# Windowed attention on quarter tiles: row-quarter scores, channel-major attended values, weights normalised before the transpose

## The chip, the core and the metric

One core of a Trainium2 chip runs the whole program. The time is device microseconds from start to end, the median of several executions. A profile is one further execution, taken by the hardware profiler. TensorE (PE) multiplies from SBUF into PSUM banks; VectorE (DVE), ScalarE (ACT) and GpSimd (POOL) do the elementwise work; SyncE (SP) issues the transfers. Each engine works through its own instructions in order and waits on semaphores for the others. TensorE's clock has two levels, 2.4 and 1.2 GHz, which the profile shows as a granted clock of 1.00 or 0.50.

## The reference

A network of five parts on 64 x 8192 inputs; after the first, each adds its result to h (64 sequences of 128 positions with 64 channels, float32). The change concerns the second part, windowed attention with eight heads of eight channels. A window is one sequence of 128 positions:

```python
qkv = xw @ qkv_weight.T + qkv_bias
q, k, v = (qkv[0], qkv[1], qkv[2])
attn = jnp.einsum('whqd,whkd->whqk', q * scale, k)
attn = attn + jnp.transpose(rpb, (2, 0, 1))[None]
attn = jax.nn.softmax(attn, axis=-1)
out = jnp.einsum('whqk,whkd->wqhd', attn, v).reshape(Bb * nW, WINDOW, C)
out = out @ proj_weight.T + proj_bias
```

The other parts are a convolutional tokenizer with its own attention, a slice attention, a bidirectional GRU with gates, and eight experts of which two are used.

## The kernel before

The stages run one after the other: 1a and 1b (convolutions and channel attention), 2 (this attention), 3 (slice attention), 4 and 5 (norm and GRU), 6 (gates), 7 (experts). Two sequences lie side by side in one 128-partition tile, a lane `l`; 32 such pairs make the stage. `stage2_pe`, `stage2_dve`, `stage2_act` and `stage2_pool` are the four engines' programs. Each has a function `slot(i, t)` that is run for t = 0 to 7 in 17 rounds i by `pipelined` (GpSimd has a loop of its own). A slot is a unit: a quarter of the 2 x 8 heads of a pair, so four heads and their 128 x 512 scores; four slots are one pair, and a round two. The order within a slot is fixed by hand, and each engine handles in one slot units of different age: `back(i, t, d)` names the unit d slots ago.

For a pair, GpSimd scales the centred rows of h (`rows`, L504), TensorE transposes them (L552), ScalarE copies them (L622), and TensorE makes queries, keys and values (L558 to L560). GpSimd spreads the keys: for each unit it multiplies them with a mask so that each head's rows stand alone in a 128 x 512 tile (`spread`, L512). For a unit, TensorE multiplies queries and spread keys (L571), VectorE adds the position bias and finds the smallest value, the scores being negated (L679), ScalarE takes the exponential in place (L646), TensorE transposes the four 128 x 128 weights into one of banks 4 to 7 (L583), VectorE copies them out (L688), and TensorE multiplies them with the values (L608). The values carry a column of ones per head, so that product also gives the softmax sum; VectorE takes its reciprocal (L697) and scales the heads' results (L700). Once a pair TensorE transposes those (L592), ScalarE copies (L656), TensorE projects and adds the bias (L598, L599), and VectorE adds to h (L692). `centre`, `square`, `variance` and `rsqrt` prepare the next stage's norm once a round.

Of the kernel before, what the change touches and what calls it, by code (L numbers as in the profile page):

```python
# [59 lines left out]
def build(nc, xp, consts, out):  # L60
# [109 lines left out]
    def stage1a_dve(v):  # L170
# [9 lines left out]
        def turn(i, g):  # L180
            if g == 0:
                max1(i, 1)
                if isinstance(i, int) and i == JA // 2 - 1:

                    v.wait_ge(loaded, 16)
                    setup3_rows_dve(v)

                    nc.vector.tensor_scalar(a_bqs[:, :], c("a_bq"), -HD ** -0.5, None, ALU.mult).then_inc(a_setup, 1)
                    nc.vector.tensor_scalar(c("a_bias"), c("a_bias"), -1.0, None, ALU.mult).then_inc(a_setup, 1)
            elif not isinstance(i, int) or i < JA // 2 - 1:  # L190
                max1(i + 1, 0)
            else:
                setup3_middle_dve(v)
# [262 lines left out]
    a_v = lane(512, 2 * 168)  # L456
    a_kz = lane(1024, 2048)
    a_o, a_oT = lane(5136, 128), lane(5264, 128)
# [27 lines left out]
    def pipelined(engine, slot):  # L486

        for t in range(8):
            slot(0, t)
        with engine.Fori(1, N2 - 1) as i:  # L490
# [6 lines left out]

    def stage2_pool(pool):
        def rows(i, l, first=False):
            n = i * 2 + (l + 1)  # L500
            if not first:
# [5 lines left out]
        def spread(i, l):  # L507


            for u in range(4):  # L510
                pool.wait_ge(a_k_r, i * 2 + (l + 1))
                nc.gpsimd.tensor_tensor(a_kz[l][:, 512 * u:512 * (u + 1)].rearrange("p (h k) -> p h k", h=4),  # L512
                                        a_k[l].unsqueeze(1).to_broadcast([128, 4, 128]),
                                        c("a_mask", 4 * u, 4 * u + 4).unsqueeze(2).to_broadcast([128, 4, 128]), ALU.mult).then_inc(a_kz_r, 1)
# [4 lines left out]

        rows(0, 0, True)  # L520
        rows(0, 1, True)
        spread(0, 0)
        for i in (1, 2):
            rows(i, 0)
            spread(i - 1, 1)
            rows(i, 1)
            spread(i, 0)
        with pool.Fori(3, N2) as i:
            finish(i - 3)
            rows(i, 0)  # L530
            spread(i - 1, 1)
            rows(i, 1)
            spread(i, 0)
        spread(N2 - 1, 1)

        pool.wait_ge(ln_rstd, LN[1] + 1)
        pool.wait_ge(a_t_r, NP)
        pool.wait_ge(f_still, 4)
        stage3_pool(pool, start=0)
        finish(N2 - 3)  # L540
        finish(N2 - 2)
        stage3_pool(pool, start=1)
        finish(N2 - 1)

    def stage2_pe(pe):
        def rows(i, l):
# [4 lines left out]
            pe.wait_ge(a_oT_r, i * 2 + (l + 1))  # L551
# [9 lines left out]

        def slot(i, t):
            l, u = t // 4, t % 4
            if exists(i, 0):
                if u == 0:
                    pe.wait_ge(a_q_r, i * 2 + (l + 1))
                pe.wait_ge(a_kz_r, i * 8 + (t + 1))
                if t >= 2 or exists(i, -1):

                    pe.wait_ge(a_mx_r, i * 8 + (t - 1))  # L570
# [1526 lines left out]
```

## Time and profile before

| | |
|---|---|
| median of 3 executions | 1465.39 us (1465.26 to 1466.63) |
| the profiled execution | 1466.03 us, span 1464.2 us |
| busy share of the span | PE 92%, DVE 66%, ACT 54%, POOL 39% |
| stage 2 | first row transposes at 231.6 us, last projection at 580.3 us |
| mean granted clock | 0.949 |

TensorE records every float32 product as two matmuls and a float32 transpose as one. A record's duration includes its way through the array; the next starts before it ends, so the pace is read from start to start. The same holds, to a smaller degree, for ScalarE and VectorE. A number behind x counts records.

### The profile page before, as it was taken

To read this page: it belongs to the slowest core of one execution; us is meant where nothing else is said; L and a number is where in the kernel's file an instruction comes from. 1 tells how busy PE (TensorE), PEld (TensorE's weight loads), DVE (VectorE), ACT (ScalarE), POOL (GpSimd) and SP (SyncE) were. 2 spreads that over 40 slices of the span, in tenths; PEclk is the share of its full clock that TensorE was granted. 3 is DMA by queue.
4 is the path that set the end of the run, shared out by engine and by line. 5 is a ranking of instruction groups with operands and counts; after the bars stand their busy time and mean duration, and the time that the engine had idled before them with its cause. 6 is when DMAs were issued, how large, how long until landed. Compare 5 with 4: busy or idle time off the path is not lost.

```text
span 1464.2 us, 42346 instructions
## 1 busy us (share of the span) xinstructions
PE 1352.3 (92%) x15300; PEld 969.4 (66%) x15300; DVE 969.7 (66%) x3518; ACT 788.6 (54%) x2105; POOL 569.1 (39%) x902
## 2 busy tenths in 40 slices
PE   6998998999999997999999998899999999969997
PEld 2446876777777776777777776456666665446665
DVE  3775776888888887687887785235555555646664
ACT  3974664556555554445545544235555555634553
POOL 5000114454445453355565554213333333225554
PEclk9988998999999998999999999569999999969999
DMA  8300000000000000000000000000000000000001
GB/s 223 74 1 0 1 1 1 1 0 0 0 0 0 0 0 1 2 2 0 0 0 0 0 0 2 0 1 1 0 0 0 0 0 1 1 1 10 15 14 23
DMA packets 9965, 13.76 MB, mean 9 GB/s; under 512 B 9008, under 2 KB 9008, under 8 KB 9392
## 3 DMA queue, kind: packets, MB, share of 16 engines
q1 hardware_dynamic: 9904, 12.93, 3.6%
q8 instruction: 40, 0.66, 0.2%
q14 instruction: 21, 0.17, 0.0%
HBM read 10.83 MB, written 2.10 MB: 9 GB/s over the span
## 4 chain that ended last, share of the span: by engine, by line
PE 75%; DVE 11%; issue 6%; ACT 6%; POOL 1%; DMA 1%; DVEq 0%; ACTq 0%; POOLq 0%; SPq 0%
PE bank L608 7%; PE bank L1267 6%; PE bank L571 6%; PE bank L1604 4%; PE bank L1622 4%; PE bank L145 4%; PE bank L1261 4%; PE bank L583 3%; PE bank L956 3%; PE bank L1226 3%; PE bank L1291 2%; PE bank L983 2%; PE bank L323 2%; PE bank L164 2%; PE bank L1369 2%
## 5 line engine op out<-in xcount | busy, mean ns | idle before, releaser
L512 POOL TENSOR_TENSOR big<-big,cst 128x512 f32<-128x512 f32 x128 | 131.9, 1062 | 131.7 <-DVE big L669 131.7
L646 ACT ACTIVATE big<-big 128x128 f32<-128x128 f32 x512 | 160.3, 391 | 33.6 <-DVE big L679 33.6
L679 DVE CUSTOM_DVE_ANT_0 big<-bank,cst 128x128 f32<-128x128 f32 x512 | 117.7, 285 | 43.3 <-issue 43.3
L571 PE MATMUL bank<-big 128*128 128x512 f32 x256 | 135.9, 613 | 1.7 <-POOL big L512 1.7
L608 PE MATMUL bank<-big 128*128 128x96 f32 x1024 | 132.2, 272 | 0.0
L608 PEld LDWEIGHTS bank<-big 128*128 128x128 f32 x1024 | 124.3, 192 | 0.9 <-issue 0.8
L1339 POOL TENSOR_TENSOR big<-g_a,g_b 64x64 f32 x128 | 40.1, 313 | 189.9 <-DVE g_a L1329 189.9
L878 POOL TENSOR_TENSOR big<-big 128x512 f32<-128x512 f32 x64 | 65.6, 1045 | 117.4 <-DVE big L1132 117.4
L1658 ACT ACTIVATE big<-bank 128x512 f32<-128x512 f32 x128 | 66.2, 603 | 51.9 <-PE bank L1604 51.9
L1320 DVE SCALAR_TENSOR_TENSOR g_t<-bank,cst,g_r 128x64 f32<-128x64 f32 x128 | 36.3, 283 | 85.6 <-ACT g_r L1306 85.6
L583 PEld LDWEIGHTS bank<-cst,big 128*128 128x128 f32 x512 | 62.5, 141 | 43.4 <-issue 37.6
L1525 POOL TENSOR_TENSOR big<-big 128x512 f32<-128x512 f32 x48 | 61.0, 1270 | 76.2 <-DVE big L1728 73.5
L266 POOL TENSOR_TENSOR eps_var<-rowsq,eps 128x4 f32 (+3 forms) x48 | 9.6, 200 | 207.6 <-DVE rowsq L262 207.6
L1291 PE MATMUL bank<-cst 128*128 128x256 f32 (+1 forms) x256 | 88.3, 426 | 0.0
L688 DVE COPY big<-bank 128x512 f32<-128x512 f32 x128 | 87.6, 684 | 0.1
L1306 ACT ACTIVATE g_r<-bank,g_bias 128x64 f32<-128x64 f32 x128 | 40.1, 313 | 87.5 <-PE bank L1267 87.5
L1267 PEld LDWEIGHTS bank<-g_b,cst 128*64 128x64 f32 x1024 | 40.3, 136 | 60.3 <-DVE g_b L1327 59.9
L1082 ACT COPY big<-bank 128x512 f32<-128x512 f32 x64 | 38.2, 597 | 73.6 <-PE bank L965 73.6
L583 PE MATMUL bank<-cst,big 128*128 128x128 f32 x512 | 77.3, 273 | 0.0
L1622 PEld LDWEIGHTS bank<-cst,big 128*64 128x64 f32 x2048 | 63.4, 140 | 19.3 <-issue 17.4
L145 PE MATMUL bank<-big,w1s 96*128 96x512 f32 x128 | 61.1, 634 | 13.8 <-DMA big<-x_dram 11.9
L1261 PE MATMUL bank<-big,cst 128*128 (+1 forms) x192 | 67.6, 440 | 1.4 <-ACT big L1235 1.4
(265 smaller groups left out, 3428.3 us busy)
## 6 DMA issues: line engine op xcount, KB each, us to landing
big<-x_dram SPq DMA_DIRECT2D x12, 512.0 KB, 8.2
cst<-consts_dram SPq DMA_DIRECT2D x1, 3364.5 KB, 22.8
out_dram<-h SPq DMA_DIRECT2D x8, 256.0 KB, 2.6
cst<-consts_dram SPq DMA_DIRECT2D x3, 256.0 KB
cst<-consts_dram SPq DMA_DIRECT2D x1, 279.5 KB, 3.9
cst<-consts_dram SPq DMA_DIRECT2D x8, 2.0 KB
cst<-consts_dram SPq DMA_DIRECT2D x2, 4.0 KB
```

The costliest lines, as they stand in the source:

```text
L145: m = nc.tensor.matmul(T(0, 2 * (q % 2) + b), w1s[0:96, 128 * g:128 * (g + 1)], xin[w][:, (2 * q + b) * 512:(2 * q + b + 1) * 512], start= ...
L512: nc.gpsimd.tensor_tensor(a_kz[l][:, 512 * u:512 * (u + 1)].rearrange("p (h k) -> p h k", h=4), a_k[l].unsqueeze(1).to_broadcast([128, 4, ...
L571: nc.tensor.matmul(bank(t % 2), a_q[l], a_kz[l][:, 512 * u:512 * (u + 1)], start=True, stop=True).then_inc(a_sc_r, 1)
L583: m = nc.tensor.transpose(bank(4 + tb % 4)[:, 128 * k:128 * (k + 1)], a_P[tb % 4][:, 128 * k:128 * (k + 1)], eye)
L608: m = nc.tensor.matmul(bank(4 + tb % 4)[:, 96 * k:96 * (k + 1)], a_PT[tb % 4][:, 128 * k:128 * (k + 1)], a_v[tb // 4][:, at + 9 * k:at + 9 ...
L646: m = nc.scalar.activation(P, P, ACT.Exp, bias=a_mx[tb % 4][:, k:k + 1], scale=-1.0)
L679: m = nc.vector.tensor_tensor_reduce(a_P[t % 4][:, 128 * k:128 * (k + 1)], bank(t % 2)[:, 128 * k:128 * (k + 1)], c("a_bias", 512 * (u % 2 ...
L688: nc.vector.tensor_copy(a_PT[tb % 4], bank(4 + tb % 4)).then_inc(a_ptc_r, 1)
L1261: nc.tensor.matmul(T(group, gate)[:, w * half:w * (half + 1)], c("g_ih", 128 * gate, 128 * gate + 128), big1[:, bass.ds(first * B + w * ha ...
L1267: m = nc.tensor.matmul(to[64 * d:64 * d + 64, :], c("g_hh", 128 * gate + 64 * d, 128 * gate + 64 * d + 64), state[:, :], start=start, stop ...
L1291: nc.tensor.matmul(T(1 - u, 3)[:, 128:384 if more else 512], c("g_hh", 0, 128), c("m_w1", 0, 256 if more else 384), start=True, stop=True, ...
L1622: m = nc.tensor.matmul(out_bank(e)[64 * half:64 * half + 64, 64 * (2 * p + s):64 * (2 * p + s) + 64], hidden(e, s)[:, 128 * p + 64 * half: ...
```

## The change

Everything is within stage 2 and its constants.

- **Scores.** GpSimd multiplies the keys with a mask of four columns (`a_mask4`) once a pair, and the result serves all four units. A unit's scores are one matmul of 32 rows, the quarter u of queries and keys. They go to banks 0, 1, 5, 7 in turn, and are issued two at a time in the odd slots, one and two slots ahead.
- **Softmax.** ScalarE's exponential also writes its sum. VectorE takes the reciprocal one slot after the scores' minimum, and GpSimd scales the weights in place (`normed`) before they are transposed.
- **Transposes.** All go to bank 4. VectorE copies the even units' out, ScalarE the odd ones'.
- **Attended values.** The values lie zero-padded in 32 columns a head. Four matmuls a unit write the four column quarters of bank 6, channel by position; the transpose of the heads is gone. ScalarE copies the 128 x 512 once a pair.
- **Projection.** It takes that layout with padded weights (`a_proj_padded`), in eight matmuls of 64 x 64; GpSimd has added the bias to h beforehand, ahead of its row scaling.
- **Setup.** Eight small transfers for the padded weights, one memset, one mask sum.

```diff
-    a_v = lane(512, 2 * 168)
-    a_kz = lane(1024, 2048)
...
+    a_v, a_kz = lane(512, 512), lane(1024, 512)
+    a_oT = lane(1536, 512)
     def four(at, cols):
         return [big[k // 2][:, at + cols * (k % 2):at + cols * (k % 2 + 1)] for k in range(4)]
-    a_P, a_PT, a_mx, a_rs = four(3072, 512), four(4096, 512), four(5120, 4), four(5128, 4)
-    a_bqs, a_pb = sb("a_bqs", [128, 1]), sb("a_pb", [128, 128])
...
+    a_P, a_PT, a_mx, a_rs, a_sm = four(3072, 512), four(4096, 512), four(5120, 4), four(5128, 4), four(5136, 4)
...
-    def pipelined(engine, slot):
-        for t in range(8):
...
+    def pipelined(engine, slot, ahead=1):
+        for i in range(ahead):
+            for t in range(8):
+                slot(i, t)
+        with engine.Fori(ahead, N2 - 1) as i:
...
+    SBANK = (0, 1, 5, 7)
+    def scores_bank(t):
+        return bank(SBANK[t % 4])
     def stage2_pool(pool):
         def rows(i, l, first=False):
             n = i * 2 + (l + 1)
+            hp = h[:, bass.ds(i * 4 + 2 * l, 2), :]
+            nc.gpsimd.tensor_tensor(hp, hp, a_pb[:, :].rearrange("p (b c) -> p b c", c=C), ALU.add)
...
-            for u in range(4):
-                pool.wait_ge(a_k_r, i * 2 + (l + 1))
...
+            pool.wait_ge(a_k_r, i * 2 + (l + 1))
+            if l or exists(i, -1):
+                pool.wait_ge(a_sc_r, i * 8 + 4 * l)
+            nc.gpsimd.tensor_tensor(a_kz[l].rearrange("p (h k) -> p h k", h=4), a_k[l].unsqueeze(1).to_broadcast([128, 4, 128]),
+                                    a_m4[:, :].unsqueeze(2).to_broadcast([128, 4, 128]), ALU.mult).then_inc(a_kz_r, 1)
+        def normed(i, t):
+            pool.wait_ge(a_rs_r, i * 8 + (t + 1))
+            P = a_P[t % 4].rearrange("p (j k) -> p j k", j=4)
+            nc.gpsimd.tensor_tensor(P, P, a_rs[t % 4].unsqueeze(2).to_broadcast([128, 4, 128]), ALU.mult).then_inc(a_n_r, 1)
         def finish(i):
             rsqrt(pool, i + (LN[1] + 1), i * 4, 4)
+        def slot(i, t):
+            l, u = t // 4, t % 4
+            if u == 2 and exists(i, l, N2 - 1):
+                spread(i + l, 1 - l)
+            ib, tb = back(i, t, 1)
+            if exists(ib, 0):
+                normed(ib, tb)
+            if u == 3 and exists(i, 1):
+                rows(i + 1, l)
+            if t == 1 and exists(i, -2):
+                finish(i - 2)
...
-            pe.wait_ge(a_oT_r, i * 2 + (l + 1))
...
+        def scores(i, t):
+            l, u = t // 4, t % 4
+            if u == 0:
+                pe.wait_ge(a_q_r, i * 2 + (l + 1))
+                pe.wait_ge(a_kz_r, i * 2 + (l + 1))
+            if t >= 4 or exists(i, -1):
+                pe.wait_ge(a_mx_r, i * 8 + (t - 3))
+            r = slice(32 * u, 32 * u + 32)
+            nc.tensor.matmul(scores_bank(t), a_q[l][r, :], a_kz[l][r, :], start=True, stop=True).then_inc(a_sc_r, 1)
+        def attended(i, t):
+            l, u = t // 4, t % 4
+            if u % 2:
+                pe.wait_ge(a_pta_r, i * 4 + (t // 2 + 1))
+            else:
+                pe.wait_ge(a_ptd_r, i * 4 + (t // 2 + 1))
+            if u == 0:
+                pe.wait_ge(a_v_r, i * 2 + (l + 1))
+                pe.wait_ge(a_oT_r, i * 2 + (l + 2))
+            for j in range(4):
+                m = nc.tensor.matmul(bank(6)[32 * j:32 * j + 32, 128 * u:128 * u + 128], a_v[l][:, 128 * u + 32 * j:128 * u + 32 * j + 32],
+                                     a_PT[t % 4][:, 128 * j:128 * j + 128], start=True, stop=True)
+            m.then_inc(a_av_r, 1)
+        def project(i, l):
+            pe.wait_ge(a_oT_r, i * 2 + (l + 1))
+            pe.wait_ge(a_h_r, i * 2 + (l + 1))
+            for s in range(2):
+                for g in range(2):
+                    for half in (0, 64):
+                        m = nc.tensor.matmul(bank(3)[half:half + 64, 128 + 64 * s:192 + 64 * s],
+                                             a_oT[l][:, 128 * (2 * s + g) + half:128 * (2 * s + g) + half + 64], a_pp[:, 64 * g:64 * g + 64],
+                                             start=(g == 0), stop=(g == 1))
+            m.then_inc(a_pr_r, 1)
         def slot(i, t):
             l, u = t // 4, t % 4
-            if exists(i, 0):
-                if u == 0:
...
             if u == 0 and exists(i, l, N2 - 1):
                 rows(i + l, 1 - l)
             if u == 1 and exists(i, l, N2 - 1):
                 qkv(i + l, 1 - l)
+            ib, tb = back(i, t, 3)
+            if exists(ib, 0):
+                attended(ib, tb)
+            if t % 2:
+                for d in (1, 2):
+                    if exists(i, (t + d) // 8):
+                        scores(i + (t + d) // 8, (t + d) % 8)
+            if u == 0 and exists(i, -1, N2 - 1):
+                project(i, l)
             ib, tb = back(i, t, 2)
             if exists(ib, 0):
-                pe.wait_ge(a_e_r, ib * 8 + (tb + 1))
-                if tb >= 4 or exists(ib, -1):
...
+                pe.wait_ge(a_n_r, ib * 8 + (tb + 1))
+                if tb % 2:
+                    pe.wait_ge(a_ptd_r, ib * 4 + (tb // 2 + 1))
+                elif tb or exists(ib, -1):
+                    pe.wait_ge(a_pta_r, ib * 4 + tb // 2)
                 for k in range(4):
-                    m = nc.tensor.transpose(bank(4 + tb % 4)[:, 128 * k:128 * (k + 1)], a_P[tb % 4][:, 128 * k:128 * (k + 1)], eye)
+                    m = nc.tensor.transpose(bank(4)[:, 128 * k:128 * (k + 1)], a_P[tb % 4][:, 128 * k:128 * (k + 1)], eye)
                 m.then_inc(a_pt_r, 1)
-            if u == 3:
-                ij, lj = (i, 0) if l else (i - 1, 1)
...
             if isinstance(i, int) and i == N2 and t < 2:
...
-            for s in range(2):
-                m = nc.scalar.copy(a_v[l][:, 168 * s:168 * s + 72].rearrange("p (h d) -> p h d", h=8)[:, :, 0:8],
...
+            nc.scalar.copy(a_v[l].rearrange("p (h d) -> p h d", d=32)[:, :, 0:8],
+                           bank(2)[:, 256:384].rearrange("p (h d) -> p h d", d=8)).then_inc(a_v_r, 1)
...
-                    m = nc.scalar.activation(P, P, ACT.Exp, bias=a_mx[tb % 4][:, k:k + 1], scale=-1.0)
+                    m = nc.scalar.activation(P, P, ACT.Exp, bias=a_mx[tb % 4][:, k:k + 1], scale=-1.0, accum_out=a_sm[tb % 4][:, k:k + 1])
...
-            if u == 3:
+            ib, tb = back(i, t, 2)
+            if tb % 2 and exists(ib, 0):
+                act.wait_ge(a_pt_r, ib * 8 + (tb + 1))
+                nc.scalar.copy(a_PT[tb % 4], bank(4)).then_inc(a_pta_r, 1)
+            if u == 2:
                 ij, lj = (i, 0) if l else (i - 1, 1)
                 if exists(ij, 0):
-                    act.wait_ge(a_ot_r, ij * 2 + (lj + 1))
-                    nc.scalar.copy(a_oT[lj], bank(2)[:, 384:512]).then_inc(a_oT_r, 1)
+                    act.wait_ge(a_av_r, ij * 8 + (4 * lj + 4))
+                    if exists(ij, -1):
+                        act.wait_ge(a_pr_r, ij * 2 + (lj - 1))
+                    nc.scalar.copy(a_oT[lj], bank(6)).then_inc(a_oT_r, 1)
...
+                if t >= 4 or exists(i, -1):
+                    v.wait_ge(a_pt_r, i * 8 + (t - 3))
                 nc.vector.memset(spare[:, 24 + t:25 + t], 0.0)
                 for k in range(4):
-                    m = nc.vector.tensor_tensor_reduce(a_P[t % 4][:, 128 * k:128 * (k + 1)], bank(t % 2)[:, 128 * k:128 * (k + 1)],
+                    m = nc.vector.tensor_tensor_reduce(a_P[t % 4][:, 128 * k:128 * (k + 1)], scores_bank(t)[:, 128 * k:128 * (k + 1)],
                                                        c("a_bias", 512 * (u % 2) + 128 * k, 512 * (u % 2) + 128 * (k + 1)), 1.0, 3e38,
                                                        ALU.add, ALU.min, a_mx[t % 4][:, k:k + 1])
                 m.then_inc(a_mx_r, 1)
             if u == 1 and exists(i, l, N2 - 1):
                 keys(i + l, 1 - l)
-            ib, tb = back(i, t, 2)
-            if exists(ib, 0):
...
             if u == 0 and exists(i, -1, N2 - 1):
                 v.wait_ge(a_pr_r, i * 2 + (l - 1))
                 hp = h[:, bass.ds(i * 4 + (2 * l - 4), 2), :]
                 nc.vector.tensor_tensor(hp, hp, bank(3)[:, 128:256].rearrange("p (b c) -> p b c", c=C), ALU.add).then_inc(a_h_r, 1)
-            ib, tb = back(i, t, 3)
+            ib, tb = back(i, t, 1)
             if exists(ib, 0):
-                v.wait_ge(a_av_r, ib * 8 + (tb + 1))
-                res = bank(4 + tb % 4)[:, 0:384].rearrange("p (j y) -> p j y", y=96)
...
+                v.wait_ge(a_e_r, ib * 8 + (tb + 1))
+                nc.vector.reciprocal(a_rs[tb % 4], a_sm[tb % 4]).then_inc(a_rs_r, 1)
+            ib, tb = back(i, t, 2)
+            if tb % 2 == 0 and exists(ib, 0):
+                v.wait_ge(a_pt_r, ib * 8 + (tb + 1))
+                if tb >= 4 or exists(ib, -1):
+                    v.wait_ge(a_av_r, ib * 8 + (tb - 3))
+                nc.vector.tensor_copy(a_PT[tb % 4], bank(4)).then_inc(a_ptd_r, 1)
...
+        o = AT["a_p"][0]
+        for k in range(8):
+            sp.dma_start(a_pp[32 * (k % 4):32 * (k % 4) + 8, 64 * (k // 4):64 * (k // 4) + 64],
+                         consts[8 * k:8 * k + 8, o:o + 64]).then_inc(m_loaded, 16)
```

TensorE, four slots of stage 2's loop. Tiles big1 and big2 are the lanes. Before, slots 1 and 2 of a round (with the semaphore arithmetic between):

```order
L571 MATMUL bank0<-big1 128x512
L558 MATMUL bank0<-big2,cst 128x128
L559 MATMUL bank0<-big2,cst 128x128
L560 MATMUL bank0<-cst,big2 128x128
L578 REGISTER_ALU
L581 REGISTER_ALU
L583 MATMUL bank1<-cst,big2 128x128 x4
L608 MATMUL bank1<-big2 128x96 x4
L567 REGISTER_ALU
L571 MATMUL bank0<-big1 128x512
```

After, slots 0 (its end) and 1:

```order
L610 MATMUL bank0<-a_proj_padded,big1 64x64 x8
L632 ISA
L638 MATMUL bank1<-cst,big2 128x128 x4
L572 MATMUL bank0<-big2,cst 128x128
L573 MATMUL bank0<-big2,cst 128x128
L574 MATMUL bank0<-cst,big2 128x128
L592 REGISTER_ALU
L598 MATMUL bank1<-big2 32x128 x4
L583 ISA
L585 MATMUL bank1<-big1 128x512 x2
L632 REGISTER_ALU
L638 MATMUL bank1<-cst,big2 128x128 x4
```

The attended values (L598, before L608) now stand ahead of the scores, and the scores (L585, before L571) ahead of the transposes (L638, before L583).

GpSimd, one lane in the loop. Before, the row scaling and the four spreads:

```order
L504 TENSOR_TENSOR big1<-xc,rstd 128x128
L511 ISA
L512 TENSOR_TENSOR big2<-big2,cst 128x512 x4
L504 ISA
L504 TENSOR_TENSOR big2<-xc,rstd 128x128
```

After, from the spread of slot 2 to the scaling of the next lane's first unit:

```order
L521 TENSOR_TENSOR big2<-big2,a_mask4 128x512
L525 REGISTER_ALU
L527 TENSOR_TENSOR big1<-big1 128x512
L525 REGISTER_ALU
L527 TENSOR_TENSOR big2<-big2 128x512
L509 ISA
L509 TENSOR_TENSOR h<-h,a_pb 128x128
L512 ISA
L513 ISA
L513 TENSOR_TENSOR big1<-xc,rstd 128x128
L527 TENSOR_TENSOR big2<-big2 128x512
```

The row scaling (L513, before L504) now stands behind a unit's scaling (L527) and the addition to h (L509).

## Rows read from the trace of the kernel before

**Rows 1.** Busy time by engine in one round of stage 2, with granted clock (PEclk).

```profile
core 0: us, PE busy (x) PEld busy (x) DVE busy (x) ACT busy (x) POOL busy (x), PEclk, DMA share, GB/s
...
260.90:281.80 20.90, 20.34 (x137) 15.94 (x135) 17.28 (x103) 12.28 (x43) 9.96 (x13) 1.00 0.00 1
```

**Rows 2.** TensorE's timeline in stage 2: start, duration, line, tiles, records.

```profile
403.19 0.27 PE L552 MATMUL bank<-cst,big 128*128 128x128 f32 x1
...
407.91 1.05 PE L571 MATMUL bank<-big 128*128 128x512 f32 x2
408.80 0.60 PE L583 MATMUL bank<-cst,big 128*128 128x128 f32 x4
409.24 1.03 PE L608 MATMUL bank<-big 128*128 128x96 f32 x8
410.10 1.05 PE L571 MATMUL bank<-big 128*128 128x512 f32 x2
```

**Rows 3.** ScalarE's timeline, the copy behind L552 of rows 2.

```profile
403.50 0.27 ACT L622 COPY big<-bank 128x128 f32<-128x128 f32 x1 [1.60 <-PE bank L552]
```

**Rows 4.** Groups by line and form: count, busy us, mean ns, idle before.

```profile
L646 ACT ACTIVATE big<-big 128x128 f32<-128x128 f32 x512 | 160.3, 391 | 33.6 <-DVE big L679 33.6
...
L1098 ACT COPY big<-bank 128x512 f32<-128x512 f32 x32 | 19.1, 598 | 0.0
...
L688 DVE COPY big<-bank 128x512 f32<-128x512 f32 x128 | 87.6, 684 | 0.1
...
L697 DVE RECIPROCAL big<-bank 128x4 f32<-128x4 f32 x128 | 22.9, 179 | 16.5 <-PE bank L608 12.6
...
L878 POOL TENSOR_TENSOR big<-big 128x512 f32<-128x512 f32 x64 | 65.6, 1045 | 117.4 <-DVE big L1132 117.4
...
L859 POOL TENSOR_TENSOR h<-h,f_bout_rows 128x128 f32 x26 | 12.0, 462 | 0.0
...
L504 POOL TENSOR_TENSOR big<-xc,rstd 128x128 f32 x26 | 10.4, 399 | 0.0
```

**Rows 5.** ScalarE's timeline in stage 1b, an exponential that also sums.

```profile
170.43 0.37 ACT L437 ACTIVATE big<-bank,big 128x128 f32<-128x128 f32 x1
170.70 0.19 ACT L437 ACTIVATION_READ_ACCUMULATOR big<-bank,big 128x1 f32 x1
170.79 0.36 ACT L437 ACTIVATE big<-bank,big 128x128 f32<-128x128 f32 x1
```

**Rows 6.** TensorE's timeline in stage 7, row halves (64*128) and column halves (128*64).

```profile
1351.80 1.99 PE L1604 MATMUL bank<-big,cst 64*128 64x512 f32 x8
1353.72 2.08 PE L1622 MATMUL bank<-cst,big 128*64 128x64 f32 x64
1355.73 1.99 PE L1604 MATMUL bank<-big,cst 64*128 64x512 f32 x8
```

**Rows 7.** TensorE's timeline in stage 1b, around a pair of column halves (L356).

```profile
169.87 0.44 PE L356 MATMUL bank<-big 128*64 128x128 f32 x4
170.24 0.44 PE L363 MATMUL bank<-cst,big 128*128 128x128 f32 x2
170.51 1.08 PE L323 MATMUL bank<-big,cst 128*128 128x256 f32 x4
...
172.32 0.61 PE L346 MATMUL bank<-big 128*128 128x128 f32 x4
172.86 0.44 PE L356 MATMUL bank<-big 128*64 128x128 f32 x4
```

**Rows 8.** TensorE's timeline, the first scores of stage 2.

```profile
236.72 2.05 PE L571 MATMUL bank<-big 128*128 128x512 f32 x2 [1.73 <-POOL big L512]
```

**Rows 9.** Windows of four other stretches, columns as in rows 1.

```profile
100.00:125.00 25.00, 19.47 (x75) 12.68 (x74) 14.00 (x33) 8.27 (x19) 1.49 (x4) 0.57 0.00 1
...
935.00:950.00 15.00, 15.00 (x61) 7.54 (x57) 5.70 (x5) 5.97 (x5) 3.06 (x5) 0.50 0.00 0
...
1100.00:1200.00 100.00, 96.61 (x1140) 65.39 (x1136) 52.31 (x240) 58.00 (x197) 30.60 (x98) 1.00 0.00 0
...
1262.00:1300.00 38.00, 31.93 (x131) 17.96 (x129) 28.58 (x76) 22.62 (x30) 12.19 (x14) 0.88 0.00 1
```

More of the change, by code:

```diff
@@ L522, in stage2_pool @@
         spread(0, 0)
[L523 to L543, printed above, removed]
+        pipelined(pool, slot, ahead=2)
     def stage2_pe(pe):
@@ L584, in slot @@
                 m.then_inc(a_pt_r, 1)
-            if u == 3:
-                ij, lj = (i, 0) if l else (i - 1, 1)
-                if exists(ij, 0):
-                    if exists(i, l):
-                        pe.wait_ge(a_v_r, i * 2 + (l + 2))
-                    pe.wait_ge(a_o_r, ij * 8 + (4 * lj + 4))
-                    nc.tensor.transpose(bank(2)[:, 384:512], a_o[lj], eye).then_inc(a_ot_r, 1)
-            if u == 0 and exists(i, -1, N2 - 1):
-                pe.wait_ge(a_oT_r, i * 2 + (l + 2))
-                pe.wait_ge(a_h_r, i * 2 + (l + 1))
-                nc.tensor.matmul(bank(3)[:, 128:256], a_oT[l], c("a_p"), start=True, stop=False)
-                nc.tensor.matmul(bank(3)[:, 128:256], eye, a_pb[:, :], start=False, stop=True).then_inc(a_pr_r, 1)
@@ L600, in slot @@
-            ib, tb = back(i, t, 3)
-            if exists(ib, 0):
-                pe.wait_ge(a_ptc_r, ib * 8 + (tb + 1))
-                if tb % 4 == 0:
-                    pe.wait_ge(a_v_r, ib * 2 + (tb // 4 + 1))
-                at = 168 * (tb % 4 // 2) + 36 * (tb % 2)
-                for k in range(4):
-                    m = nc.tensor.matmul(bank(4 + tb % 4)[:, 96 * k:96 * (k + 1)], a_PT[tb % 4][:, 128 * k:128 * (k + 1)],
-                                         a_v[tb // 4][:, at + 9 * k:at + 9 * k + 96], start=True, stop=True)
-                m.then_inc(a_av_r, 1)
@@ L616, in stage2_pe @@
         pe.wait_ge(f_dve, SETUP3)
+        pe.wait_ge(m_loaded, LOADED7)
+        scores(0, 0)
+        scores(0, 1)
         pipelined(pe, slot)
@@ L812, in setup3_last_pe @@
         pe.wait_ge(f_dve, 16)
-        pe.wait_ge(m_made, 2)
+        pe.wait_ge(m_made, 3)
         nc.tensor.matmul(T(1, 0)[:, 0:128], mean_of[:, :], f_bd[:, :], start=True, stop=True)
@@ L1820, in _ @@
         def _(pool):
+            nc.gpsimd.memset(a_pp[:, :], 0.0).then_inc(m_made, 1)
             nc.gpsimd.memset(c("m_b2"), 0.0).then_inc(m_made, 1)
@@ L1885, in _ @@
             for l in range(2):
-                nc.vector.memset(a_v[l], 1.0).then_inc(a_ones, 1)
-            v.wait_ge(a_setup, 2)
+                nc.vector.memset(a_v[l], 0.0).then_inc(a_ones, 1)
+            v.wait_ge(a_setup, 3)
             stage2_dve(v)
```

53 lines of the change are left out of this document (21 added, 32 removed).

## The prediction

> **What bounds the kernel now.** I read the windows of the attention stage first. It runs from 231 to 583 us: 16 rounds of eight slots, one slot for a quarter of the heads (a unit). A steady round takes 20.9 us, TensorE is busy 20.3 of them, and the granted clock is 1.00 [rows 1]. Then the TensorE timeline inside a round: the scores take 0.89 us (407.91 to 408.80), the transposes 0.44, the attended values 0.86, and the next slot starts 2.19 after this one [rows 2]. So TensorE sets the pace. I count in groups of four slots, of which the stage has 32: 10.45 us each.
>
> **What the change takes from TensorE.** Scores become 32-row matmuls, two adjacent ones on different row quarters and banks. The nearest row is the 64-row pair of the last stage: eight records of 512 columns, four matmuls, in 1.92 us from start to start [rows 6], so 0.43 to 0.48 each where the whole array pays 0.89. Attended values become four matmuls of 32 columns side by side. The nearest row is again there: 64 records of 64 columns on alternate halves in 2.01 us, so one starts every 31 ns while one alone needs about 55. Eight records of 128 columns on four quarters would then take 0.22; with no overlap they would be the old 0.86. I take 0.22. The projection goes from 0.45 to 16 half-array records, about 0.5 by that row. The transpose of the heads goes.
>
> Against it stands the change of tile shape. Transposes and products use the whole array, attended values a column quarter, scores a row quarter, projection a half: 11 changes in a group. Four transposes before a half-array pair take 0.54 instead of 0.44, the pair takes 0.37 instead of 0.22, and the two transposes behind it 0.27 instead of 0.22 [rows 7]. That is 0.30 for two changes, 0.15 each. The Trainium skill (TensorEngine Tiling (Array Packing), Key Properties) says that changing the tiling mode drains the engine; by that alone a change has no price, and the sum of a group would be 1.6 us lower on TensorE, but the trace shows the 0.15. The Trainium skill (TensorE: Matmul & The Clock Gate, Part 3: Packing small matmuls) also says that weight loads overlap running matmuls only when the row group differs; that would deny the four column quarters their overlap, and it speaks against this change. By [rows 6] it does not hold for halves, whose records alternate at 31 ns.
>
> TensorE's own work in a group is then: scores 1.75, transposes 1.76, attended 0.9, projection 0.5, row products 0.8, changes 1.65: 7.4 us of 10.45. TensorE no longer bounds at full clock.
>
> **What it adds elsewhere, per group.** ScalarE: the exponentials now write their sum. In the convolution stage such an exponential is followed by a read of the accumulator, and the next starts 0.36 after it [rows 5]; the ones here read SBUF and are a little longer (0.391 against 0.37, [rows 4, 5]), so 0.385 each, 1.54 a unit, 1.64 to the end of the last read. Two weight copies of 512 columns and one of the attended values come to it, 0.60 each with the next start after 0.50 [rows 4]. ScalarE's sum: 6.16 + 1.5 + 0.8 for small copies like [rows 3] = 8.45. VectorE loses two copies and the scaling of 0.2 a unit, and falls to about 6.5. GpSimd spreads one quarter of the keys instead of four (saves 3 x 1.04) and gets four scalings of 512 columns at 1.04 (the same form as L878) and one addition to h at 0.42 (0.46 with the overlap, L859), before the row scaling of 0.40: 6.7. No engine's sum reaches 10.45.
>
> **But the units are chained.** What was a wait that TensorE's queue covered is now a loop through four engines, since all transposes share bank 4 and each engine takes its work in order. Followed through one group (handoffs 0.04 as between L552 and L622, [rows 2, 3], 0.08 into GpSimd):
>
> - ScalarE: exp of unit 1 1.54, copy of the attended values 0.50, exp of unit 2 1.68 with handoff: 3.72.
> - VectorE reciprocal 0.17 (179 ns in [rows 4]) + 0.08, then GpSimd scales unit 2 for 1.04, adds to h for 0.42 and scales the next rows for 0.40 + 0.04: 2.15. The addition to h stands ahead of the rows that TensorE waits for.
> - TensorE transposes the rows 0.31, ScalarE copies them 0.16: 0.47. That wait of TensorE holds up all behind it in its queue.
> - ScalarE exp of unit 3 1.68, reciprocal 0.12, VectorE copy of unit 2's weights 0.69 + 0.04: 2.53.
> - TensorE: attended values of unit 2 0.22 + 0.15, both scores 0.86 + 0.15 (they stand ahead of the transposes), transposes of unit 3 0.61 to the end + 0.04 + 0.15; ScalarE's copy 0.50: 2.65, rounding once.
>
> Sum 11.52; every second group has the square of the norm, 0.3 more: 11.67 on average, or 1.22 over 10.45. Times 32 = 39 us. Removed work on TensorE is thus hidden anyway: 1466.0 (the profiled execution; 0.6 over the median) + 39 = **1505 at full clock**. With a shorter sum on ScalarE (0.36) and cheap changes the group is 11.3 and the time 1493; I see no lower end above the rival below. Setup (eight small transfers queued on SP behind the large constants, a memset, a mask reduction) is worth nothing: TensorE first waits for x, issued ahead of them, and the stage begins at 231 us. They would cost their issue, under 3 us, if x of the third quarter waited for them.
>
> **The clock is the larger term.** TensorE would be at 7.4 of 11.67, on tiles that fill a quarter of the array for the scores. In the trace, stretches with a gappy TensorE didn't keep 1.00: 78% busy from 100 to 125 us had 0.57, 84% from 1262 to 1300 had 0.88, and from 935 to 950, after an idle stretch, one half-array product after another was busy throughout and stayed at 0.50 [rows 9]. At 1.2 GHz columns cost double: the first scores of the stage took 2.05 for what takes 1.05 [rows 2, 8]. A group held at that level: scores 3.4, transposes 3.4, attended 1.8, rows and products 1.5, projection 0.9, changes at 0.2 each 2.2, and three times a bare handoff transposes, copy, attended with nothing of TensorE's own between (0.95 each): 16.0. TensorE would be the bound and stay below the full clock. The stage begins below it too [rows 8]. Between 11.67 and 16.0 I take the middle, an estimate: TensorE falls when a group is thin and rises when scores, attended values and products crowd. 13.75 - 10.45 = 3.3; x 32 = 105; **1571 us**.
>
> **The rivals.**
> - Full clock throughout: 1505. For it: the recurrent stage keeps 1.00 with half-array products, though with filler products between them. Against it: [rows 9].
> - The lower level nearly throughout: 16.0 x 32 gives 1466 + 178 = 1644. For it: 935 to 950. Against it: transposes and products still use the whole array.
> - The tiles don't overlap, so the change doesn't do what it says: scores 0.89 and attended 0.86 stay, and in the chain they add 0.9 + 0.64. 13.2 a group: 1466 + 88 = 1554 at full clock. Against it: [rows 6].
> - Faster: the chain is looser than I draw it, because each engine runs ahead of the others by a unit. Then ScalarE's sum of 8.45 is the bound: 32 x 2.0 = 64 less, 1402. It decides where handoffs hide more than 1.22 us a group. For it: four score banks instead of two, and scores issued a slot or two early. Against it: one transpose bank, and three of the four exponentials lie on the chain with GpSimd's 1.04 between.
>
> **How the numbers follow.** Mixed clock 0.52 (1530 to 1615), full clock 0.22, lower level 0.10, tiles serial 0.05, faster 0.08, and within 0.2%, which is about what a measurement of this kernel can tell from no change, 0.03. The time is the likeliest one's, 1571. The range leaves out the faster cases and most of the lowest clock: 1494 to 1620. Faster by over 0.2%: 0.08; within: 0.03; slower: 0.89.
>
> **What would show it.** The attention stage should last some 380 us at full clock and 450 at a mixed one, with granted clocks between 0.5 and 1 in its windows. Scores should start in pairs, attended values in fours. Exponentials should start 0.385 apart. GpSimd should wait for the reciprocal; VectorE's reciprocal for the exponential; TensorE's row transposes for GpSimd's row scaling; TensorE should be idle before the attended values. A stage under 350 us with a busy ScalarE would prove the chain wrong; a steady 1.00 would prove the clock wrong and leave 1505.

## The result, and the profile after

The changed kernel takes 1563.54 us (median of 4 runs, 1563.24 to 1565.22), the kernel before on the same chip 1465.33. That is 1.0678 times as long, with a 95% interval of 1.0655 to 1.0702. The forecast was 1571, the range 1494 to 1620. The page of the changed kernel (busy time by engine, then the granted clock in 40 slices of 39 us):

```profile
PE 1353.4 (87%) x15652; PEld 903.9 (58%) x15652; DVE 911.6 (58%) x3327; ACT 872.2 (56%) x2649; POOL 617.2 (40%) x967
...
PEclk9988996677777777769999999856999999989999
```

The loss lies in the seventh to eighteenth slices, the attention stage, from its first row transposes at 231.4 to its last projection at 678.9 us. Its pace can be read off ScalarE's copy of the transposed rows, which comes once in a group of four slots. Here are the copies of before (L622), all 32 and then the sixth to the thirtieth; behind them those of after (L654) and the windows of the same stretch (columns as in [rows 1]):

```profile
L622 ACT COPY big<-bank x32: 265/265/267, 233.0 to 551.5; 128x128 f32<-128x128 f32 x32
...
L622 ACT COPY big<-bank x25: 265/265/267, 276.6 to 530.4; 128x128 f32<-128x128 f32 x25
```

```profile
L654 ACT COPY big<-bank x32: 266/266/272, 232.9 to 644.3; 128x128 f32<-128x128 f32 x32
...
L654 ACT COPY big<-bank x25: 266/266/272, 290.4 to 617.1; 128x128 f32<-128x128 f32 x25
...
290.00:618.00 328.00, 244.99 (x1913) 144.66 (x1914) 163.06 (x1092) 211.47 (x931) 157.24 (x192) 0.75 0.00 0
```

24 groups in 326.7 us are 13.61 each, against (530.4 - 276.6) / 24 = 10.57 before. From the first copy to the last it is 411.4 against 318.5, a difference of 93 of the 98 us. TensorE, busy 20.34 of 20.90 us in [rows 1], is now busy three quarters of the time, at a mean clock of 0.75. Four stretches of 6.8 us show how that mean comes about:

```profile
397.10:403.90 6.80, 5.80 (x45) 4.13 (x47) 2.80 (x20) 3.78 (x19) 2.45 (x5) 0.50 0.00 0
404.00:410.80 6.80, 4.24 (x36) 1.88 (x32) 3.70 (x30) 4.82 (x20) 4.80 (x7) 0.99 0.00 0
410.80:417.60 6.80, 6.11 (x47) 4.13 (x47) 3.17 (x16) 3.79 (x19) 2.62 (x4) 0.51 0.00 0
417.60:424.40 6.80, 4.16 (x36) 1.88 (x32) 3.92 (x29) 5.12 (x21) 3.13 (x4) 1.00 0.00 0
```

The clock changes between its two levels, 1.2 and 2.4 GHz, and one turn of it is one group long. The clock keeps to this turn from 294 us to the end of the loop. At the upper level TensorE has gaps (4.2 of 6.8 us busy), and the clock then falls; at the lower it is busy for 5.8 to 6.1 of 6.8, and the clock then rises. TensorE's timeline through one turn (start, duration, line, tiles, records, idle time before with its releaser):

```profile
405.82 0.43 PE L598 MATMUL bank<-big 128*32 128x128 f32 x8 [0.67 <-ACT big L685]
406.18 0.66 PE L638 MATMUL bank<-cst,big 128*128 128x128 f32 x4
408.17 0.43 PE L598 MATMUL bank<-big 128*32 128x128 f32 x8 [1.33 <-DVE big L736]
408.53 1.13 PE L585 MATMUL bank<-big 32*128 32x512 f32 x4
409.59 0.66 PE L638 MATMUL bank<-cst,big 128*128 128x128 f32 x4
411.49 0.48 PE L566 MATMUL bank<-cst,big 128*128 128x128 f32 x1 [1.25 <-POOL big L513]
...
413.53 1.12 PE L638 MATMUL bank<-cst,big 128*128 128x128 f32 x4
...
415.86 0.66 PE L598 MATMUL bank<-big 128*32 128x128 f32 x8
416.44 1.64 PE L585 MATMUL bank<-big 32*128 32x512 f32 x4
```

The gaps are waits for the copies (L685, L736) and for GpSimd's row scaling (L513). The waits of 300 to 560 us (total, times, longest), the longest sums first:

```profile
POOL big L527 <- DVE big L730: 130.1, 78, 2.9
DVE h L726 <- PE bank L610: 56.9, 19, 3.2
ACT big L685 <- PE bank L638: 56.5, 38, 2.4
DVE big L730 <- ACT big L676: 44.1, 39, 1.8
PE bank L566 <- POOL big L513: 26.3, 19, 1.6
```

Each engine of the loop waits for the one ahead of it: GpSimd's scaling (L527) for the reciprocal (L730), the reciprocal for the exponential (L676), and ScalarE's copy (L685) for the transposes (L638).

### The profile page after: what moved, and what is told of

Its sections match the earlier page's. It is cut to its first block, busy times and chain, and to the rows that moved or that the text cites. A ratio compares the mean times of both kernels' runs of the same rounds, so it can differ in the third digit from the quotient of the medians.

```text
span 1561.5 us, 43734 instructions
## 1 busy us (share of the span) xinstructions
PE 1353.4 (87%) x15652; PEld 903.9 (58%) x15652; DVE 911.6 (58%) x3327; ACT 872.2 (56%) x2649; POOL 617.2 (40%) x967
## 4 chain that ended last, share of the span: by engine, by line
PE 55%; issue 20%; POOL 9%; DVE 9%; ACT 5%; POOLq 1%; DMA 1%; DVEq 0%; ACTq 0%; SPq 0%
PE bank L1302 6%; POOL big L527 4%; PE bank L1639 4%; PE bank L1657 4%; PE bank L145 4%; PE bank L1296 4%; PE bank L1261 2%; PE bank L991 2%; PE bank L1326 2%; PE bank L1018 2%; PE bank L324 2%; POOL big L521 2%; PE bank L164 2%; PE bank L1404 2%; PE bank L1059 2%
## 5 line engine op out<-in xcount | busy, mean ns | idle before, releaser
L527 POOL TENSOR_TENSOR big<-big 128x512 f32<-128x512 f32 x128 | 133.3, 1041 | 220.5 <-DVE big L730 220.5
L676 ACT ACTIVATE big<-big 128x128 f32<-128x128 f32 x512 | 198.5, 393 | 1.3 <-DVE big L717 1.3
L598 PE MATMUL bank<-big 128*32 128x128 f32 x1024 | 70.1, 357 | 66.1 <-DVE big L736 42.9
L913 POOL TENSOR_TENSOR big<-big 128x512 f32<-128x512 f32 x64 | 65.7, 1047 | 113.3 <-DVE big L1167 113.3
L638 PEld LDWEIGHTS bank<-cst,big 128*128 128x128 f32 x512 | 66.0, 165 | 68.9 <-POOL big L527 33.7
L638 PE MATMUL bank<-cst,big 128*128 128x128 f32 x512 | 103.2, 334 | 0.0
L676 ACT ACTIVATION_READ_ACCUMULATOR big<-big 128x1 f32 x512 | 98.0, 191 | 0.0
L685 ACT COPY big<-bank 128x512 f32<-128x512 f32 x64 | 37.5, 586 | 100.2 <-PE bank L638 100.2
L585 PE MATMUL bank<-big 32*128 32x512 f32 x256 | 89.6, 781 | 1.7 <-POOL big L521 1.7
L1560 POOL TENSOR_TENSOR big<-big 128x512 f32<-128x512 f32 x48 | 61.0, 1271 | 71.8 <-DVE big L1763 69.1
L598 PEld LDWEIGHTS bank<-big 128*32 128x32 f32 x1024 | 23.3, 126 | 98.0 <-ACT big L685 32.2
L1117 ACT COPY big<-bank 128x512 f32<-128x512 f32 x64 | 38.2, 597 | 73.0 <-PE bank L1000 73.0
```

Source lines behind the costliest of these rows:

```text
L527: nc.gpsimd.tensor_tensor(P, P, a_rs[t % 4].unsqueeze(2).to_broadcast([128, 4, 128]), ALU.mult).then_inc(a_n_r, 1)
L585: nc.tensor.matmul(scores_bank(t), a_q[l][r, :], a_kz[l][r, :], start=True, stop=True).then_inc(a_sc_r, 1)
L598: m = nc.tensor.matmul(bank(6)[32 * j:32 * j + 32, 128 * u:128 * u + 128], a_v[l][:, 128 * u + 32 * j:128 * u + 32 * j + 32], a_PT[t % 4][ ...
L638: m = nc.tensor.transpose(bank(4)[:, 128 * k:128 * (k + 1)], a_P[tb % 4][:, 128 * k:128 * (k + 1)], eye)
L676: m = nc.scalar.activation(P, P, ACT.Exp, bias=a_mx[tb % 4][:, k:k + 1], scale=-1.0, accum_out=a_sm[tb % 4][:, k:k + 1])
L913: nc.gpsimd.tensor_tensor(w, w, f_rs[l][:, 8 * s:8 * s + 8].unsqueeze(2).to_broadcast([128, 8, 64]), ALU.mult).then_inc(f_w_r, 1)
```

## The experiments

The theory has two terms: a loop through four engines whose group is 11.67 us, and a clock that falls in its gaps. The rivals are that the loop or the tile changes alone make the loss, or that TensorE's or ScalarE's own work does. The runs are not all on one chip, so between two of them a difference is given by their times and by their ratios to the kernel before. All times are medians of four runs beside the kernel before on the same chip.

**1. Keep TensorE busy, and change nothing else.**

```diff
+            if not isinstance(i, int):
+                k = t + 2 + t % 2
+                pe.wait_ge(a_mx_r, i * 8 + (k - 3))
+                nc.tensor.matmul(scores_bank(k)[:, 0:256], eye, c("a_bias", 0, 256), start=True, stop=True)
```

> The changed kernel with one more matmul on TensorE in each slot of rounds 1 to 14: 256 columns of a constant against the identity, on the whole array, into the score bank that is next to be overwritten, behind the transposes. It adds work (4 x 0.43 us a group at full clock) and takes none away. Theory 'clock': the granted clock in the attention stage goes to 1.00 and the group from 13.65 to 11.7 us: 1563.5 - 1.95 x 28 groups = 1509 us (1500 to 1525). Rival 'chain and tile changes alone' (the clock is only a symptom of a TensorE that waits): no gain, 1563 or up to 1.7 us a group more, 1611.

It takes 1508.6 us against 1461.8, a ratio of 1.0324 (1.0293 to 1.0355). It does more work and takes 55 us less than after (52 by the two ratios). The same rows in its trace:

```profile
L658 ACT COPY big<-bank x32: 265/265/272, 230.9 to 590.6; 128x128 f32<-128x128 f32 x32
...
L658 ACT COPY big<-bank x25: 265/265/266, 286.7 to 567.3; 128x128 f32<-128x128 f32 x25
...
286.00:568.00 282.00, 227.90 (x2113) 132.96 (x2113) 162.72 (x1092) 208.05 (x928) 158.38 (x193) 1.00 0.00 0
```

The clock is 1.00 and the group 280.6 / 24 = 11.69 us. The loop can now be walked without the clock's doing. In this kernel the lines from the extra matmul (L643) on are 4 higher: L680 is the exponential, L689 and L740 the weight copies, L734 the reciprocal, L658 the copy of the rows.

```profile
401.03 0.18 DVE L734 RECIPROCAL big<-big 128x4 f32<-128x4 f32 x1 [0.70 <-ACT big L680]
...
401.29 1.04 POOL L527 TENSOR_TENSOR big<-big 128x512 f32<-128x512 f32 x1 [1.28 <-DVE big L734]
...
402.29 0.45 POOL L509 TENSOR_TENSOR h<-h,a_pb 128x128 f32 x1
...
402.70 0.40 POOL L513 TENSOR_TENSOR big<-xc,rstd 128x128 f32 x1
...
403.23 0.32 PE L566 MATMUL bank<-cst,big 128*128 128x128 f32 x1 [1.12 <-POOL big L513]
...
403.60 0.27 ACT L658 COPY big<-bank 128x128 f32<-128x128 f32 x1 [1.29 <-PE bank L566]
403.76 0.40 ACT L680 ACTIVATE big<-big 128x128 f32<-128x128 f32 x1
...
405.44 0.18 DVE L734 RECIPROCAL big<-big 128x4 f32<-128x4 f32 x1 [0.43 <-ACT big L680]
...
405.62 0.69 DVE L740 COPY big<-bank 128x512 f32<-128x512 f32 x1
...
406.37 0.16 PEld L598 LDWEIGHTS bank<-big 128*32 128x32 f32 x8 [0.34 <-DVE big L740]
406.37 0.43 PE L598 MATMUL bank<-big 128*32 128x128 f32 x8
...
406.72 1.13 PE L585 MATMUL bank<-big 32*128 32x512 f32 x4
...
407.78 0.66 PE L638 MATMUL bank<-cst,big 128*128 128x128 f32 x4
...
408.48 0.58 ACT L689 COPY big<-bank 128x512 f32<-128x512 f32 x1 [1.28 <-PE bank L638]
...
408.96 0.40 ACT L680 ACTIVATE big<-big 128x128 f32<-128x128 f32 x1
...
410.98 0.41 ACT L680 ACTIVATE big<-big 128x128 f32<-128x128 f32 x1
...
412.66 0.18 DVE L734 RECIPROCAL big<-big 128x4 f32<-128x4 f32 x1 [0.40 <-ACT big L680]
```

From reciprocal to reciprocal, 401.03 to 412.66, it is 11.63 us, by just the stations that the prediction named. This group holds no square of the norm; the groups with it, every second one, take 11.75 to 11.76.

**2 and 3. GpSimd's row scaling first,** without and with the extra matmul.

```diff
+            if u == 3 and exists(i, 1):
+                rows(i + 1, l)
             ib, tb = back(i, t, 1)
             if exists(ib, 0):
                 normed(ib, tb)
-            if u == 3 and exists(i, 1):
-                rows(i + 1, l)
```

> The changed kernel with GpSimd's addition to h and row scaling issued ahead of the scaling of the unit in the third slot of a group, instead of behind it. Theory 'chain of the prediction' (row transposes held up by GpSimd's row scaling, everything behind them in TensorE's queue): a group loses up to 1.04 us at full clock, and about half of it while the clock alternates: 1530 to 1550. Theory 'the group is locked to the alternation of the clock': within 8 us of 1563. Rival 'row transposes are not on the chain': no change, and none in the next run either.

> Both edits: the extra matmul in each slot and GpSimd's row scaling ahead of the unit's. If the row scaling is on the chain at full clock, the group is 1.0 us shorter than with the extra matmul alone: about 10.7 us and 1480 (1465 to 1495). If it isn't, the same time as with the extra matmul alone, 1509.

Alone it takes 1566.7 us, ratio 1.0717 (1.0694 to 1.0739), which is no gain. With the extra matmul it takes 1477.4, ratio 1.0105 (1.0083 to 1.0126), 31 us under run 1. The rows, first of the edit alone, then of both edits:

```profile
L654 ACT COPY big<-bank x25: 271/271/272, 288.4 to 615.8; 128x128 f32<-128x128 f32 x25
...
288.00:616.00 328.00, 273.61 (x1900) 155.42 (x1900) 164.35 (x1092) 208.13 (x927) 157.22 (x192) 0.62 0.00 0
...
402.00:408.80 6.80, 4.79 (x41) 2.29 (x37) 3.57 (x29) 4.30 (x19) 5.58 (x8) 1.00 0.00 0
408.90:429.20 20.30, 17.81 (x122) 10.66 (x121) 9.94 (x64) 12.92 (x58) 7.42 (x9) 0.50 0.00 0
```

```profile
L658 ACT COPY big<-bank x25: 266/266/266, 283.4 to 536.7; 128x128 f32<-128x128 f32 x25
...
283.00:537.00 254.00, 222.32 (x2099) 132.36 (x2097) 163.41 (x1099) 207.11 (x927) 158.83 (x193) 1.00 0.00 0
...
409.32 0.59 PE L643 MATMUL bank<-cst 128*128 128x256 f32 x2
409.75 0.27 PE L566 MATMUL bank<-cst,big 128*128 128x128 f32 x1
```

At full clock the edit takes the group from 11.69 to 10.55 us, 1.14 less. The row transposes (L566) waited 1.12 us for the row scaling in run 1 (at 403.23), because the scaling of a unit (1.04) stood ahead of it; here they start with no wait, 0.43 after the extra matmul. So the row scaling was on the loop. Without the extra matmul the group stays at 13.64 us, since the clock is now low for 20.5 of 27.3 us, two groups, instead of for half of the time. What the loop gained, the clock took back. The theory of a group locked to the clock had foretold that the time would stay; the turn, though, is now two groups long instead of one. Why two groups again come to 27.3 us isn't settled.

**4 and 5. No softmax sums,** without and with the extra matmul. The weights are then not normalised.

```diff
-                    m = nc.scalar.activation(P, P, ACT.Exp, bias=a_mx[tb % 4][:, k:k + 1], scale=-1.0, accum_out=a_sm[tb % 4][:, k:k + 1])
+                    m = nc.scalar.activation(P, P, ACT.Exp, bias=a_mx[tb % 4][:, k:k + 1], scale=-1.0)
...
-                nc.vector.reciprocal(a_rs[tb % 4], a_sm[tb % 4])
+                nc.vector.reciprocal(a_rs[tb % 4], one[:, 0:1].to_broadcast([128, 4]))
```

> The changed kernel whose exponentials write no sums; the reciprocal is taken of ones instead, so the weights are not normalised. Each exponential then goes from 0.385 to about 0.30 us from start to start. The prediction's chain has three of the four units' exponentials on it: 3 x 0.36 = 1.0 to 1.1 us a group less, 1530; and more, down to 1505, if the shorter group also gives TensorE the higher clock for more of the time. Rival 'ScalarE is off the path, the order on TensorE and the clock set the group': within 8 us of 1563.

> Exponentials without sums (weights not normalised, reciprocal of ones) and the extra matmul of 256 columns a slot: the price of the sums at full clock, against the run with the extra matmul alone (1508.6, group 11.69). The chain of the prediction has three exponentials of a group's four on it, each unit 0.36 shorter: 1.08 a group less, 1508.6 - 1.08 x 29 = 1477. Rival 'the sums are off the path': 1508.

Alone it takes 1554.0 us, outside either expectation, ratio 1.0618 (1.059 to 1.0645). With the extra matmul it takes 1487.1, ratio 1.0158 (1.0141 to 1.0175). ScalarE's timeline in the latter, eight exponentials in a row:

```profile
402.74 2.44 ACT L680 ACTIVATE big<-big 128x128 f32<-128x128 f32 x8
```

The last of eight takes 0.39, so they start (2.44 - 0.39) / 7 = 0.293 us apart, against 0.38 to 0.39 with sums. A sum thus costs 0.09 an instruction and 0.37 a unit. The group fell from 11.69 to 10.78 us (284.2 to 543.0 in 24), by 0.91, where three units on the loop would have given 1.1; the expectation was 10 us too low. Again the low clock hides more than half of a gain: it is 9 to 10 us alone, and 21 to 24 at full clock.

**6. Scores on the whole array.** Each unit's scores sum over four quarters, so the values are others.

```diff
-            nc.tensor.matmul(scores_bank(t), a_q[l][r, :], a_kz[l][r, :], start=True, stop=True).then_inc(a_sc_r, 1)
+            nc.tensor.matmul(scores_bank(t), a_q[l], a_kz[l], start=True, stop=True).then_inc(a_sc_r, 1)
```

> The changed kernel with its scores as matmuls over all 128 rows instead of a row quarter; each unit's scores then sum over four quarters, so the values are others. TensorE's own time for them goes from 0.43 to 0.89 us a unit at full clock, 1.8 us a group more. Theory 'thin tiles cost the clock': the granted clock rises from 0.75 to above 0.8 in the attention stage, and the run is not slower and may be faster: 1535 to 1565. Rival 'TensorE's work counts as its time': two of four scores stand in the chain, 0.9 us a group more, 1592.

```profile
L654 ACT COPY big<-bank x25: 266/271/272, 286.8 to 606.3; 128x128 f32<-128x128 f32 x25
...
286.00:607.00 321.00, 254.77 (x1924) 138.42 (x1922) 162.70 (x1092) 206.63 (x929) 157.25 (x192) 0.90 0.00 0
```

It takes 1551.2 us, ratio 1.0614 (1.0579 to 1.065), 12 us less than after (9 by the ratios; the two intervals just miss each other). A pair's scores now take 1.82 us from start to start at full clock (395.97 to 397.79), where they took 1.06; the mean clock rose from 0.75 to 0.90, and the group fell from 13.61 to 13.31 us. So more work on TensorE doesn't lengthen the kernel here: what the row quarters save is more than given back through the clock. Whether the clock answers to the time that TensorE works or to how much of the array it uses, this run doesn't tell, as both rose. No run has whole-array scores at a steady clock.

**7 and 8. The same computation with later stages,** with an extra matmul of 192 columns and without. The row scaling is first, as in run 2. Transposes and copies stand three slots behind the scores, attended values four (ScalarE's copy of them one slot later too), and on TensorE the transposes come ahead of the attended values and the scores.

```diff
-            ib, tb = back(i, t, 3)
-            if exists(ib, 0):
-                attended(ib, tb)
...
-            ib, tb = back(i, t, 2)
+            ib, tb = back(i, t, 3)
             if exists(ib, 0):
                 pe.wait_ge(a_n_r, ib * 8 + (tb + 1))
...
+            ib, tb = back(i, t, 4)
+            if exists(ib, 0):
+                attended(ib, tb)
```

> The whole computation in another order: a unit's transposes and the copies of its weights stand three slots behind its scores instead of two, its attended values four instead of three, and on TensorE the transposes come ahead of the attended values and the scores of the slot. GpSimd's row scaling is first, and an extra matmul of 192 columns a slot keeps TensorE busy. The theory that the group was a loop through ScalarE, VectorE, GpSimd and TensorE says that each of them now finds its input ready a slot earlier: the group goes below the 10.56 us of the run with row scaling first and the extra matmul, to about 9.6: 1477 - 0.95 x 29 = 1450 us (1440 to 1462). Rival 'an engine's own work is the bound': 1477 stays.

> The same order without the extra matmul. Its work is smaller by 4 x 0.32 us a group on TensorE. If the clock needs that work (theory 'clock'), the granted clock leaves 1.00 again and the run is slower than with it, 1465 to 1510. If the shorter group alone keeps TensorE at full clock: the same or up to 0.16 us a group faster, 1445 to 1450.

With the extra matmul it takes 1441.3 us, ratio 0.9846 (0.9829 to 0.9862), within the expected range. Without it, it takes 1434.2, ratio 0.9813 (0.9787 to 0.9839), better than either of its two expectations. The groups are 9.57 and 9.47 us. The second, without extra work:

```profile
271.00:500.00 229.00, 191.78 (x1911) 109.30 (x1909) 159.14 (x1103) 207.18 (x932) 159.52 (x194) 0.97 0.00 0
```

Its work is that of the changed kernel, and both runs beat the kernel before. With its gaps closed the loop nearly holds the clock by itself. Run 7 against run 3 changes the slots and TensorE's order together (and the width of the extra matmul), so what each of them gives isn't separated.

**9 to 12. The row scaling in the second slot of a group,** on top of the order of run 8. Run 9 has that alone, run 10 adds an extra matmul of 64 columns, run 11 also has the copy of the attended values on VectorE, and run 12 has that copy moved but no extra matmul.

```diff
-            if u == 3 and exists(i, 1):
+            if u == 1 and exists(i, 1):
                 rows(i + 1, l)
```

> The later stages without the extra matmul, and GpSimd's addition to h and row scaling in the second slot of a group instead of the fourth, where they stood ahead of the unit TensorE waits for. ScalarE's own work in a group (8.45 us and half a square) is then the nearest bound. Group from 9.47 to about 8.95 us: 1434 - 0.5 x 29 = 1419 (1412 to 1427). Rival: GpSimd's place is covered and the occasional longer groups at the lower clock remain: 1434.

> The same with an extra matmul of 64 columns a slot on TensorE. If groups of 11.1 us at a lower clock still turn up without it, as one in six did in the run with the later stages alone, they go and the time falls by up to 8 us, 1412 to 1420. If none is left there, the same time or 2 us more.

> The same, and the copy of the attended values out of the PSUM is VectorE's instead of ScalarE's. If ScalarE's sum is the bound, a group loses up to 0.5 us: 1403 to 1410. If the loop through the four engines still sets the pace, nothing or a little more than before, 1416 to 1424.

> The kernel with the row scaling early and no extra matmul (1420.9, group 9.01, ScalarE busy 38 of 40 us in the attention stage), with the copy of the attended values on VectorE. If ScalarE's own work is the bound, the group falls by up to 0.4 us: 1409 to 1414. If the loop sets the pace, and ScalarE only fills its waits, no gain: 1419 to 1427.

In this order they take 1420.9 us, ratio **0.9721** (0.9695 to 0.9746), as expected; 1425.4, ratio 0.9752; 1426.7, ratio 0.9763; and 1421.9, ratio 0.9736 (0.971 to 0.9763). Run 9, from the sixth copy to the thirtieth:

```profile
L654 ACT COPY big<-bank x25: 265/265/267, 272.8 to 488.9; 128x128 f32<-128x128 f32 x25
...
272.00:489.00 217.00, 184.51 (x1901) 105.02 (x1897) 158.35 (x1094) 205.34 (x929) 158.41 (x193) 1.00 0.00 0
```

A group is 216.1 / 24 = 9.00 us at a clock of 1.00. An extra matmul now buys nothing: it costs 4.5 us and makes the group 0.14 longer, where 2 us at most were expected if no low clock was left. ScalarE is busy 95% of the time, yet taking a copy of 0.57 a group off it gained nothing, with the extra matmul (1425.4 to 1426.7) and without (1420.9 to 1421.9). So its busy share did not name the bound. That the loop still sets the pace is what is left; it wasn't walked in this order.

## Why the prediction was right, point by point

- **TensorE no longer bounds: right.** In run 1, from start to start and without the extra matmul, a group has four units' attended values at 0.35, four units' scores in 2.12, four units' transposes at 0.50, and rows, projection and products in some 1.5. That is about 7.1 us, for 7.4 foretold.
- **Scores in pairs: right.** Two adjacent units' scores take 1.06 us from start to start with the change of shape (406.72 to 407.78); 1.01 was taken.
- **Attended values and the price of a shape change: right.** Eight records on four column quarters and the drain behind them take 0.35 (406.37 to 406.72), for 0.22 + 0.15. With no overlap they would be the 0.86 of before, by the prediction. This bears on the rule that the prediction weighed: the Trainium skill (TensorE: Matmul & The Clock Gate, Part 3: Packing small matmuls) has weight loads overlap only when the row group differs. The trace disagrees, since all eight records share their rows, yet their eight weight loads are over within 0.16 us beside running matmuls. The drain that the Trainium skill states (TensorEngine Tiling (Array Packing), Key Properties) has a price in time here: two passes of 0.11 (the second four records start 0.11 after the first four) leave 0.13 of the 0.35 for it.
- **The chain: right, to 0.02 us in its mean,** 11.67 against 11.69. Walked once, without the square of the norm, it is 11.63 for 11.52. Its stations: exponential, copy, exponential 3.72, measured 3.70 (408.96 to 412.66); reciprocal and GpSimd 2.15, measured 2.20; rows 0.47, measured 0.53; third exponential, reciprocal, VectorE's copy 2.53, measured 2.61; TensorE to ScalarE's copy 2.65 (its terms add up to 2.68), measured 2.59. That the mean fits to 0.02 is partly luck: the walk was 0.11 too short, and the square adds 0.12 to every second group where 0.3 was taken. That the row scaling lies on the chain, run 3 showed, by the wait of 1.12 that it removed.
- **The start of the stage: not in the sum.** From the first copy to the sixth it is 43.6 us before, 57.5 after and 55.8 in run 1. There the stage begins at the lower level, and of windows of 7 us the first above it is that from 264 to 271 us, with 0.87; before, it is that from 236 to 243, with 0.73. Five groups at 11.69 against five at 10.57 explain 5.6 of the 12.2 us that run 1 takes more there; the rest goes with the lower clock, which no run took away.
- **The clock as the larger term: right.** Run 1 puts it at 52 to 55 us of 98, and the loop and the start at 47 on that chip. The prediction had 66 and 39. Run 1 takes the clock's part out of 28 of the 32 groups only, (13.61 - 11.69) x 28 = 54; the start's share of it is in the 47. The loop by itself is (11.69 - 10.57) x 32 = 36.
- **The middle between 11.67 and 16.0: right in size, in part by luck.** Half of the time is spent at either level. If the loop went at the pace of 11.69 in the upper half, a group of 13.61 gives a lower one of 6.8 / (1 - 6.8 / 11.69) = 16.3, an estimate, for 16.0 foretold. So both ends fit, though no run held a group at the lower level, and it was right that the clock falls when TensorE is thin and rises when work crowds. That the share is one half, nothing in the prediction derived; run 2 has three quarters after a small edit. Not foreseen either was that clock and loop lock into one turn per group. The same sum for run 2, three quarters of the time low and 10.55 at the upper level, gives 0.75 x 13.64 / (1 - 0.25 x 13.64 / 10.55) = 15.1.
- **The rivals.** Full clock throughout is run 1, 1509 for 1505, and it needs the extra work. The lower level nearly throughout didn't come; it held for half of the time. Tiles that don't overlap are ruled out by the rows above. ScalarE's sum as the bound, the faster case, needed a looser chain; with later stages the kernel went to 9.0 us a group and 1421, not to 8.45 and 1402.
- **The sign of a mixed clock: right.** The stage should last some 450 us; it lasts from 231.4 to 678.9, 448.
- **Setup worth nothing: right.** The first copy is at 233.0 before and 232.9 after.

The Trainium skill (TensorE: Matmul & The Clock Gate, Part 1, HAM oscillation) describes a clock that goes up and down with waits in the program; there the waits are for DMA, here for three other engines, and the trace shows it in the four windows above.

## What to carry to other kernels

Before you take work off the engine that bounds, walk the loop that its queue has hidden, hop by hop and in each engine's own order. Here the sum of the hops, not the busiest engine, was the new period. Then ask whether TensorE keeps its clock in the gaps: an extra matmul whose result is never read, put where its bank is about to be overwritten, tells in one run how much of a loss is clock. Measure small edits with the clock held, since at an unsteady clock a shorter loop can show no gain. If the loop is the bound, move its stages a slot apart before giving the change up: here that, with the row scaling moved forward, turned 7% slower into 3% faster with the same work.

## What the hardware showed that was not expected

- The loop locked to the clock: groups of 13.61 us with the lower level for half the time, and rounds of 27.3 us again with it for three quarters, when the loop itself was 1.14 us shorter.
- Scores that take 1.82 us a pair instead of 1.06 made the kernel 9 to 12 us faster; an extra matmul of 0.43 us a slot made it 52 to 55 us faster.
- An exponential of 128 columns that also writes its sum starts the next one 0.385 us later, one that doesn't 0.293.
- Four matmuls on four column quarters with different weights all start within 0.02 us in the records, the second four 0.11 after the first (run 1).
